# Channels 4 to 7 of the input turned by VectorE in 32x32 squares instead of by TensorE

## What is computed

```python
x = x + L0(_gn(x))      # mlp: per channel e, gelu(x @ w1[e] + b1[e]) @ w2[e] + b2[e]
x = x + L1(_gn(x))      # 3x3 conv over 8 channels, binarized weights
x = x + L2(_gn(x))      # mlp, tanh gelu
x = x + L3(_gn(x))      # mlp, exact gelu
# x: (2, 8, 256, 256) = batch, channel, token, feature;  w1[e]: 256x1024;  w2[e]: 1024x256
# _gn: group norm over pairs of channels and all tokens and features, eps 1e-5
```

## Time and profile before

| | us |
|---|---|
| median of three timed runs | 608.18 (605.89 to 608.58) |
| the profiled execution | 611.48 |
| its span, first to last instruction | 609.7 |
| TensorE busy | 592.4 (97%) |
| VectorE busy | 426.7 (70%) |
| ScalarE busy | 419.1 (69%) |

### The profile page before, as it was taken

One profiled execution on the slowest core, in us unless ns is written; L12 is line 12 of the kernel. 1 busy time (PEld: TensorE's weight loads), 2 busy tenths in 40 slices (PEclk: granted clock), 3 DMA queues, 4 the chain that ended last, 5 costly groups with the idle time before them and its releaser, 6 DMA issues.

```text
span 609.7 us, 8604 instructions
## 1 busy us (share of the span) xinstructions
PE 592.4 (97%) x2905; PEld 497.3 (82%) x2905; DVE 426.7 (70%) x887; ACT 419.1 (69%) x705; POOL 36.7 (6%) x57
## 2 busy tenths in 40 slices
PE   7989999999999988999999999999999999999997
PEld 7768888888889756988888888888888888888887
DVE  5885998867667977796965866866775675675632
ACT  4867767677767652687767777777777777777753
POOL 2000000000000670000000000000000000000000
PEclk9989999999999997999999999999999999999999
DMA  8843455364353393441422323223234234234001
GB/s 281 279 143 106 129 166 177 106 179 147 111 175 104 81 146 97 143 139 69 129 81 85 122 70 131 77 74 134 70 105 137 88 111 148 87 103 156 19 18 69
DMA packets 56909, 73.04 MB, mean 120 GB/s; under 512 B 4217, under 2 KB 50459, under 8 KB 56866
## 3 DMA queue, kind: packets, MB, share of 16 engines
q1 hardware_dynamic: 54262, 70.31, 37.9%
q10 hardware_dynamic: 2604, 2.19, 1.8%
HBM read 59.71 MB, written 8.59 MB: 112 GB/s over the span
## 4 chain that ended last, share of the span: by engine, by line
PE 85%; DMA 5%; DVE 5%; ACT 2%; issue 1%; POOL 1%; SPq 0%; ACTq 0%; DVEq 0%; POOLq 0%
PE G L1079 40%; PE ACC L1099 13%; PE ACC L1104 13%; PE ACC L1100 13%; PE ACC L1131 2%; DMA XT<-XC 1%; PE ACC L1150 1%; DVE BN L741 1%; PE TR L1162 1%; DMA W2raw<-in_L_conv_w 1%; DMA W1raw<-in_L_conv_w 1%; DMA NAT<-in_x 1%; DMA XC<-x_scratch 1%; DVE Cl L892 1%; ACT HR L637 1%
## 5 line engine op out<-in xcount | busy, mean ns | idle before, releaser
L816 DVE TENSOR_TENSOR Hl<-HR,Hh 128x512 fp32r<-128x512 f32 (+1 forms) x208 | 134.1, 645 | 157.2 <-ACT Hh L641 156.3
L637 ACT ACTIVATE HR<-G,BT 128x512 f32<-128x512 f32 (+1 forms) x208 | 136.2, 655 | 141.1 <-PE G L1079 141.0
L1079 PE MATMUL G<-Xh,W1l 128*128 128x512 f32 (+1 forms) x416 | 160.5, 386 | 0.1
L1079 PE MATMUL G<-Xh,W1h 128*128 128x512 f32 (+1 forms) x416 | 155.4, 374 | 0.0
L1079 PE MATMUL G<-Xl,W1h 128*128 128x512 f32 (+1 forms) x416 | 151.8, 375 | 0.0
L1099 PE MATMUL ACC<-Hh,W2l 128*128 128x512 f32 (+1 forms) x400 | 147.7, 373 | 0.2 <-issue 0.2
L1100 PE MATMUL ACC<-Hh,W2h 128*128 128x512 f32 (+1 forms) x400 | 147.5, 372 | 0.0
L641 ACT ACTIVATE Hh<-HR 128x512 fp32r<-128x512 f32 (+1 forms) x208 | 124.7, 600 | 6.6
L1104 PE MATMUL ACC<-Hl,W2h 128*128 128x512 f32 (+1 forms) x400 | 116.8, 373 | 0.4 <-DVE Hl L816 0.3
L1079 PEld LDWEIGHTS G<-Xh,W1h 128*128 128x128 f32 x416 | 78.6, 189 | 14.1
L1079 PEld LDWEIGHTS G<-Xh,W1l 128*128 128x128 f32 x416 | 78.7, 189 | 12.8 <-ACT HR L637 0.2
(11 more groups left out here) (95 smaller groups left out, 403.4 us busy)
## 6 DMA issues: line engine op xcount, KB each, us to landing
W2raw<-in_L_conv_w SPq DMA_DIRECT2D x23, 1024.0 KB, 5.6
W1raw<-in_L_conv_w SPq DMA_DIRECT2D x34, 512.0 KB, 4.5
W1raw<-in_L_conv_w SPq DMA_DIRECT2D x7, 1024.0 KB, 5.1
XC<-x_scratch SPq DMA_DIRECT2D x16, 304.0 KB, 6.1
x_scratch<-XT SPq DMA_DIRECT2D x16, 256.0 KB
out_x<-OUTT SPq DMA_DIRECT2D x16, 256.0 KB, 2.1
NAT<-in_x SPq DMA_DIRECT2D x6, 512.0 KB, 9.2
XT<-XC SPq DMA_DIRECT2D x16, 112.0 KB
```

Of the source, the lines that this page charges most:

```text
L637: nc.scalar.activation(HR[:, u % 2, 0:n], G1[u % 2][:, 0:n], act_of_layer, bias=BT1[:, f, col:col + 1]).then_inc(gelu_done, 1)
L816: nc.vector.tensor_tensor(Hl[:, u % RING, 0:n], HR[:, u % 2, 0:n], Hh[:, u % RING, 0:n].bitcast(F32), ALU.subtract).then_inc(hlo, 1)
L1079: ins = nc.tensor.matmul(G1[u % 2][:, 0:n], w[:, par, c, col], rhs, start=i == 0, stop=i == len(parts) - 1)
```

## The change

Channels 0 to 3 are handled as before. For channels 4 to 7:

- `load_squares(g)` replaces `load_x(g)`, g = 2 and 3. Per channel, batch and block of 32 partitions, one transfer of 64 KB: partition 32k+j receives, for tokens 8j to 8j+7 and both feature halves, the 32 features 32k to 32k+31 of that half, in runs of 128 bytes. That is 16 transfers and 8192 runs for each g.
- `turn_in` on VectorE transposes 32x32 squares from NAT into XT: two instructions of 128x256 per channel and batch, writing every eighth token. The eight turns stand at the end of VectorE's work in units 11, 12, 13, 15 (g = 2) and 17, 19, 20, 21 (g = 3).
- TensorE's transposes of units 8 to 15 and their evacuations on ScalarE and VectorE are gone. The sums of channels 4 to 7 wait for the turns by semaphore.
- SP's order: the squares of g = 2 stand between W2 of expert 1 and W1 of expert 2, and the conv loads behind the latter. Then W2 of expert 2, the squares of g = 3, the store of channel 0, W1 and W2 of expert 3, and only then the first load of XC, which now waits for all eight turns. From E = 4 on the order is as before.

```diff
@@ -42,6 +42,10 @@
 
 GROUPS = 2
 SPAN = PART // GROUPS
+SQUARE = 32
+NSQ = PART // SQUARE
 
 KS = 3
 ROWS = PART // C
@@ -153,6 +157,8 @@
 
 SPLIT_AT = split_steps()
 WEIGHTS_AT = weight_steps()
+
+TURNS = (11, 12, 13, 15, 17, 19, 20, 21)
 
 
 
@@ -343,6 +349,7 @@
         w2_first = [sem(f"w2_first{hh}") for hh in range(2)]
         w1_in, w2_in, bias_in, conv_in = sem("w1_in"), sem("w2_in"), sem("bias_in"), sem("conv_in")
         consts, diag_zero = sem("consts"), sem("diag_zero")
+        in_turned = sem("in_turned")
         in_tr, in_evac_act, in_evac_dve = sem("in_tr"), sem("in_evac_act"), sem("in_evac_dve")
         bias_moved, bias_tr, bias1_t, bias2_t = sem("bias_moved"), sem("bias_tr"), sem("bias1_t"), sem("bias2_t")
         bn_done, mv_done, mean_mm, dm_done = sem("bn_done"), sem("mv_done"), sem("mean_mm"), sem("dm_done")
@@ -396,7 +403,7 @@
 
         def bank_of(i):
 
-            return ROT[i % 4] if i < 8 else TR
+            return ROT[i % 4]
 
         def evacuated(i):
 
@@ -414,6 +421,18 @@
                 for b in range(B):
                     sp.dma_start(NAT[:, g, b], x[b, 2 * g:2 * g + 2].rearrange("e (c p) d -> p e c d", p=PART)
                                  ).then_inc(x_in[g - 1], 16)
+
+            def load_squares(g):
+
+
+                for e in range(2):
+                    for b in range(B):
+                        for k in range(NSQ):
+                            own = x[b, 2 * g + e, 0, SQUARE * k:SQUARE * (k + 1)]
+                            runs = bass.AP(tensor=own.tensor, offset=own.offset,
+                                           ap=[[N // SQUARE * D, SQUARE], [PART, N // SQUARE * DC], [1, SQUARE]])
+                            sp.dma_start(NAT[SQUARE * k:SQUARE * (k + 1), g, b, e].rearrange("p c d -> p (c d)")
+                                         .rearrange("p (a r) -> p a r", r=SQUARE), runs).then_inc(x_in[g - 1], 16)
 
             def load_w1(E):
                 f, e = divmod(E, C)
@@ -442,10 +461,10 @@
                 sp.dma_start(W2raw[:, HT // 2 * hh:HT // 2 * (hh + 1)],
                              w2[0][0][H // 2 * hh:H // 2 * (hh + 1)].rearrange("(t p) d -> p t d", p=PART)
                              ).then_inc(w2_first[hh], 16)
-            for g in (2, 3):
-                load_x(g)
             load_w1(1)
             load_w2(1)
+            load_squares(2)
+            load_w1(2)
 
             for i in range(C):
                 sp.dma_start(conv_rep[i:PART:C], cw[:, i].rearrange("o a b -> o (a b)").unsqueeze(0)
@@ -469,7 +488,7 @@
             def load_xc(e, bs, stored, value, done):
 
                 if e == 0:
-                    sp.wait_ge(in_tr, B * C)
+                    sp.wait_ge(in_turned, B * C // 2)
                 sp.wait_ge(stored, value)
                 for b in bs:
                     first = x1_dram[e, 0:ROWS, b * N:(b + 1) * N]
@@ -485,13 +504,16 @@
                     sp.dma_start(XT[GROUPS * i + g:GROUPS * (i + n):GROUPS, c, :, b],
                                  XC[j * C:(j + n) * C, b, own.start, 1:N + 1]).then_inc(x2_in[b], 16)
 
-            for E in range(2, C + 1):
-                if E >= 3:
-                    store_x1(E - 3, BOTH, x1_out)
+            load_w2(2)
+            load_squares(3)
+            for E in range(3, C + 1):
+                store_x1(E - 3, BOTH, x1_out)
                 load_w1(E)
-                if E >= 3:
+                if E > 3:
                     load_xc(E - 3, BOTH, x1_out, 80 * (E - 2), xc_in)
                 load_w2(E)
+                if E == 3:
+                    load_xc(E - 3, BOTH, x1_out, 80 * (E - 2), xc_in)
             store_x1(C - 2, BOTH, x1_out)
             load_xc(C - 2, BOTH, x1_out, 80 * (C - 1), xc_in)
             for b in range(B):
@@ -709,8 +731,6 @@
                     w_hi(*weight)
                 if u in SPLIT_AT:
                     x_hi(*SPLIT_AT[u])
-                if E == 1 and t % 2 == 0:
-                    x_evac(8 + t)
                 if E > 2 * C and t in (5, 7):
                     out_evac_step(E - 1, (t - 5) // 2)
             act.wait_ge(final_done, 1)
@@ -727,11 +747,23 @@
                 nc.vector.tensor_copy(XT[:, :, e, b], bank_of(i)[:].rearrange("p (c n) -> p c n", c=DC)
                                       ).then_inc(in_evac_dve, 1)
 
+            def turn_in(g, i):
+
+                e, b = divmod(i, B)
+                if i == 0:
+                    dve.wait_ge(x_in[g - 1], 16 * 2 * B * NSQ)
+                src = NAT[:, g, b, e].rearrange("p c d -> p (c d)").rearrange("p (s c r) -> p c s r", c=DC, r=SQUARE)
+                for c in range(DC):
+                    ins = nc.vector.transpose(XT[:, c, 2 * g + e, b].rearrange("p (i s) -> p s i", i=SQUARE), src[:, c])
+                ins.then_inc(in_turned, 1)
+
             def sums(J, channels=(0, 1)):
 
                 e, bs, of, steps = JOBS[J]
                 for b in bs:
                     for i in channels:
+                        if of == -1 and e >= 4:
+                            dve.wait_ge(in_turned, 2 * e - 4)
                         if of == 0:
                             dve.wait_ge(evicted, evicted_by(pass_of(e + i, b)))
                         elif of == 0.5:
@@ -1002,8 +1034,8 @@
                     x_lo(*SPLIT_AT[u])
                 if u == unit(FINAL - 1, 6):
                     add_final_bias()
-                if E == 1 and t % 2 == 1:
-                    x_evac(8 + t)
+                if u in TURNS:
+                    turn_in(*divmod(TURNS.index(u) + 4 * B, 2 * B))
                 if E == 1 and t == 6:
                     signs_and_means()
                     bias_of_next()
@@ -1022,16 +1054,10 @@
                 e, b = divmod(i, B)
                 if i < 2 * B:
                     pe.wait_ge(x_first[i], 16)
-                elif i % (2 * B) == 0:
-                    pe.wait_ge(x_in[e // 2 - 1], 32)
-
-                if 4 <= i < 8:
+                elif i == 2 * B:
+                    pe.wait_ge(x_in[0], 32)
+                if i >= 4:
                     pe.wait_ge(in_evac_act, i - 3)
-                if i == 8:
-                    pe.wait_ge(bias1_t, 1)
-                    pe.wait_ge(bias2_t, LAYERS)
-                if i > 8:
-                    pe.wait_ge(*evacuated(i))
                 dst = bank_of(i)
                 for c in range(DC):
                     for r in range(NC):
@@ -1212,8 +1238,6 @@
                     mean_over_partitions(J)
                 for J in jobs_at("variance", u):
                     variance_over_partitions(J)
-                if E == 1:
-                    x_transpose(8 + t)
                 if E > 2 * C and t in (4, 6):
                     out_transpose(E - 1, t // 2 - 2)
             for u in (UNITS - 2, UNITS - 1):
```

## The result

The changed kernel took 624.66 us (median of four, 622.11 to 625.51) against 607.03 us for the kernel before beside it: a ratio of 1.028, 95% interval 1.024 to 1.033. The prediction said 613.0 and at most 621. The direction and both places were right, the sizes were not: the first load cost 6.2 us where 3.4 were forecast, the second 9.3 where 4.7 were.

The account below looks back on a forecast made before the run. The prediction took TensorE, busy 97% of the span, plus its few waits as the bound. Removed transposes -3.3, first load +3.4 and second load +4.7 gave +4.8 us on 608.18, so 613.0 us, range 607 to 621.

Parts of the forecast that it names:

- the first load: W1 of expert 2, queued behind 16 square transfers on SP, lands at 41.7 us and delays TensorE: +3.4 us.
- What is removed: TensorE's transposes in units 8 to 15: seven groups of 0.47 us count, 3.3 us gained.
- rivals 1 and 2: Squares ahead of W1 of expert 2: slow feed, sum +12.3 us, chance 0.12; size floor, sum +11.1 us, chance 0.08.
- rival 2: Squares' transfers: a 128-byte run costs what one of 512 would; W1 of expert 2 +9.7, sum +11.1 us, chance 0.08.
- What else queues on SP is moved without price: Conv loads, W2 of expert 2, second squares, store of channel 0 and W1 of expert 3 move later on SP, costing nothing.
- The turn: VectorE's two 128x256 transposes per channel and batch take 0.7 us, bounds 0.5 and 1.3.
- That alone TensorE bears: Pass 2: four turns make VectorE 2.8 us late, Hl of unit 21 is 2.1 late, and TensorE bears that.
- The second load: XC waits for all eight turns ahead of W1 of expert 4, which lands at 96.2 us: +4.7 us.
- Rival 5: Slow transposes: VectorE needs 1.3 us a turn, sum +7.2 us, 615.4, chance 0.05.
- Rivals 3 and 4: Both loads: shallow waits, sum +1.2 us, 609.4, chance 0.24; both land in time, 604.9, chance 0.09.

Follow-up runs that it names:

- gaps: Changed kernel with turns of channels 6 and 7 and XC loads later, squares in eights where SP had waited, conv loads behind W2 of expert 2: ratio 0.995.
- sixteen: Changed kernel with its 16 transfers each moving 64 runs of 1 KB, single execution: TensorE waited 4.1 us before the mean matmul, against 8.2 in the change.
- W1 first: Changed kernel with W1 of expert 2 issued before the squares of channels 4 and 5: ratio 1.030.
- twice: Kernel before the change with the TensorE transposes of channels 4 to 7 done twice: ratio 1.002.
- both: Changed kernel with W1 of expert 2 before the squares and the first XC load behind W1 of expert 4: ratio 1.016.
- plain loads: Changed kernel with two plain 512 KB loads of 1 KB runs in place of each group of 16 square transfers: ratio 1.011.
- XC later: Changed kernel with the first load of XC issued behind W1 of expert 4: ratio 1.013.

## Why the prediction was wrong

**What is removed.** Right: 0.47 us per group, seven groups, 3.3 us. Five of them show as -2.3 from unit 11 to 16; the other two lie inside the stretch of the first wait.

**The first load.** The mechanism was right, the place, the order and TensorE following. Mis-sized is the issue: 0.64 us was taken, 0.755 was paid (12.08 for 16; over all 32 the median is 0.63, the dearest 1.37). With that alone the load is 1.9 us later, 5.3 in place of 3.4; measured, W1h of expert 2 began 5.6 us later than before, counted from unit 8. The price of a run was right. The DMA view of the change for 33.5 to 38 us:

```profile
DMA packets 3577, 0.45 MB, mean 101 GB/s; under 512 B 3576, under 2 KB 3576, under 8 KB 3576
...
q1 hardware_dynamic: 3576, 0.44, 67.4%
```

67.4% of 16 engines over 4.5 us for 3576 packets is 13.6 ns each, where the line between the earlier trace rows gave 13.8. That also ends rivals 1 and 2: 795 packets per us went through, not 457, and a run of 128 bytes doesn't cost what one of 512 would (27 ns by the prediction's line). The Trainium skill ("DMA: Bandwidth & Descriptors", Specifications) puts the smallest transfer at line rate at 512 bytes. As far as bandwidth goes the trace agrees: 101 GB/s at 67% busy in this stretch, an estimated 150 at full share, against the 384 GB/s of that of the earlier trace rows. The trace contradicts only the reading that each small run would pay for 512 bytes, which is rival 2's and goes further than that row of the page.

What I left out of this term is the clock. The windows of the change (granted clock third from the end):

```profile
46.00:49.00 3.00, 0.00 (x0) 0.00 (x0) 2.97 (x5) 1.72 (x3) 0.00 (x0) 0.50 0.27 63
...
54.00:56.00 2.00, 2.00 (x7) 1.66 (x6) 1.45 (x3) 0.73 (x2) 0.12 (x1) 0.50 0.60 98
56.00:58.00 2.00, 2.00 (x10) 1.62 (x9) 0.00 (x0) 0.61 (x1) 0.58 (x1) 1.00 0.51 78
```

The clock stands at 0.50 (1.2 GHz) from 45.9 on, during the idle time, to about 56. Before the change matmuls ran at that level from about 42.7 to 46.0, here from 49.5 to 56.0: unit 10 to 11 took 1.1 us more than before, though it had lost a group. The idle time alone doesn't tell how long the clock stays down: in these runs it was 3.4 us at 0.50 after 2.2 us (before) and after 3.8 ("gaps"), 6.8 after 4.1 ("sixteen"), 10.2 in all around 8.2 (the change). Nor does it tell whether the clock falls: 1.61 us in "W1 first" was followed by 0.50; 1.58 in "twice", 1.71 in "both" and 1.87 in "plain loads" were not.

**"What else queues on SP is moved without price."** This sentence was true of the change and hid the real bound. In the change W2 of expert 2 landed at 52.8 and was wanted at 61.4, W1 of expert 3 landed at 68.5 and was wanted at 72.3. "W1 first" and "both" showed that this is one budget: 32 square issues (24.8 us), the conv loads (6.3 us) and the store of channel 0 (3.4 us) fill SP from 27 to 64 us, and in the orders tried who is served first only picked the load that is late. One order wasn't tried alone: W1 of expert 2 first and the conv loads behind W2 of expert 2 or W1 of expert 3, which would take 7 us from ahead of W2.

**VectorE.** The turn was mis-sized: 0.7 us was taken with the overlap of neighbours already off. Measured, a turn takes 1.16 to 1.24 us from start to end, and the next instruction starts 1.00 to 1.08 us after it does: inside the bounds (0.5 to 1.3) but about half above the value. The working was right for a dense transpose and for a strided copy; that their combination costs more no row of before could tell. Four turns take 4.2 us of VectorE and not 2.8. "That alone TensorE bears" failed with it: 1.2 us are lost between units 20 and 31 when the second wait is taken away ("XC later"), and none when the turns leave pass 2.

**The second load.** Right in its order, and mis-sized in two steps. In the times of the change, the last turn was to end at 86.8 + 5.4 = 92.2 and ended at 94.1:

```profile
92.81 1.24 DVE L757 STREAM_TRANSPOSE XT<-NAT 128x256 f32<-128x256 f32 x2
```

SP's longest waits (what it waited for, us in total, times, longest) name that turn:

```profile
SPq L497 <- DVE XT L757: 21.6, 1, 21.6
```

W1 of expert 4 was to leave at 96.5 and left at 98.73; it was to land 5.1 us later and took 7.5. The two transfers of XC and the store of channel 1 were issued in the 5 us before it, the next two of XC and W2 of expert 4 in the 5 us behind it, and the engines' share at 104 to 107 us was still 1.07; in "XC later", with none of them near, the same load took 4.8. So the weights landed 1.9 + 0.3 + 2.4 = 4.6 us later than forecast. ScalarE waited 10.3 us (6 to 7 forecast), TensorE 6.25 (2.7 forecast), and TensorE's matmuls ran at 0.50 from 107.6 to 110.6. With the turns' lateness it cost 9.3 us, not 4.7, and that lateness is the difference; "XC later" took 8.1 of them away.

**The sum.** -3.3 + 3.4 + 4.7 = +4.8 was forecast; the ledger has -2.3 + 6.2 + 9.3 = +13.1, with two of the groups inside the second figure. The range failed because each term's high bound was combined with the middle of the others, and because neither the hold of an issue nor the landing time of the second load had a high bound of its own. Rival 5 was right about its cause (VectorE slow) and half right about its size. Rivals 3 and 4 had nothing.

So two steps of the prediction failed, both in size: the issue of a square at 0.64 us with no price for a longer half clock (3.4 us forecast, 6.2 measured), and the second load, with 0.7 us a turn and 5.1 us to land (4.7 forecast, 9.3 measured).

## What to carry to other kernels

Count an issuing queue as an engine with its own busy time: issues times their held time, against the gaps between the loads that someone waits for. If that sum doesn't fit, another order of the same issues may only change which load is late, as two orders did here; fewer transfers ("plain loads") and gaps elsewhere ("gaps") did help. And before a load is made to wait for a new event, ask what stands behind it in the same queue.

## What the runs showed of the hardware

- A VectorE transpose of 128x256 float32 in 32x32 squares took 0.42 us with dense output and 0.67 us when it wrote every eighth element; a copy with that output stride took 0.43.
- An issue of 64 KB held SP 0.43 us with 1 KB runs, 0.63 with 128-byte runs, both at the median. In three early stretches, with the transfer engines busy 72 to 92%, one with 128-byte runs held it 0.99 to 1.28 us on average; the change's first 16 took 0.755 at 81%, so the share alone doesn't explain it.
- Runs of 128 bytes cost the engines 13.6 ns each (3576 of them), between the 36-byte and 288-byte rows.
- The same transfers from GpSimd left only every 2.7 to 5.8 us.
- The granted clock fell to 0.50 behind an idle time of 1.61 us in one execution and stayed at 1.00 behind 1.71 us in another of the same instructions up to there; from unit 8 to 11 the first took 1.5 us longer. A half clock behind a wait is a term that differed between executions of the same instructions here, by about 1.5 us.
- The conv stretch took between 36.2 and 42.3 us in different kernels with the same instructions there. In the kernel before VectorE waited 3.1 us in it for the last transfers back into XT, in the change 0.4, and the clock stood at 0.50 for 6.8 and 3.4 us; what makes these transfers late in one execution and not in another wasn't tried.
